# A message-passing kernel: one block per loop body in rounds two and three, its count buffer in seven parts

## The reference

```python
# L0 (round one)
agg = segment_sum(x[src], dst, n);  mean = agg / maximum(deg, 1)[:, None]
h = relu(concatenate([x, mean]) @ W_fc + b_fc) + x @ W_res + b_res
x = layernorm(x + h)
# L1 (rounds two and three), the same conv twice, relu in between
msg = x[src] @ Wm + bm + edge_attr @ We + be
out = segment_sum(msg, dst, n) + x @ Ws + bs
# at the end
x = layernorm(x + out)
```

## Time and profile before

| | |
|---|---|
| timed runs | 4176.44 us median of 3 (4168.92 to 4176.94) |
| profiled execution, first to last instruction | 4128.3 us |
| what lies around it, up to the median of the timed runs | 48.1 us |
| rounds two and three, loops | some 2382 to 3195 us, and 3285 to 4072 us |

### The profile page before, as it was taken

The page is one execution under the profiler, slowest core; times in us unless marked ns, Lnnn a source line. Parts: engine busy times, 40 slices in busy tenths (PEclk is TensorE's granted clock), DMA queues, the critical chain, the costliest instruction groups (busy, mean ns, idle before and its releaser), DMA issues.

```text
span 4128.3 us, 116481 instructions
## 1 busy us (share of the span) xinstructions
PE 3373.4 (82%) x39555; PEld 3061.4 (74%) x39555; DVE 2361.8 (57%) x5334; ACT 1654.2 (40%) x2148; POOL 1962.3 (48%) x2298
## 2 busy tenths in 40 slices
PE   0148899999999995777778888899898789889894
PEld 0137888888888885666667778888888688888884
DVE  7579888898888885777775622222222322222224
ACT  0134577789999995777775400000000300000000
POOL 7722244456666662222221355555554655555552
PEclk9879999999999998999999689999999899999997
DMA  2542355556666664666664389888987798998984
GB/s 94 91 47 104 136 198 209 206 220 248 246 239 241 251 248 157 190 187 187 186 189 126 93 318 334 332 333 328 333 331 280 235 334 326 333 331 326 335 324 148
DMA packets 321181, 967.62 MB, mean 234 GB/s; under 512 B 145354, under 2 KB 238546, under 8 KB 262190
## 3 DMA queue, kind: packets, MB, share of 16 engines
q1 hardware_dynamic: 274338, 893.02, 60.9%
q0 software_dynamic: 46784, 73.84, 6.6%
HBM read 700.07 MB, written 269.81 MB: 235 GB/s over the span
## 4 chain that ended last, share of the span: by engine, by line
PE 64%; DVE 11%; issue 11%; POOL 4%; ACT 4%; DVEq 3%; DMA 2%; ACTq 0%; another core or an unknown queue 0%; POOLq 0%; SPq 0%
PE ps L1060 45%; PE ps L1083 11%; PE ps L1052 4%; DVE union L765 3%; DVE union L878 3%; ACT union L1373 3%; PE ps L1130 2%; DVE abuf L889 2%; POOL abuf L1170 1%; DVEq L439 1%; DVEq L889 1%; PE ps L1020 1%; POOL union L1170 1%; PE ps L974 1%; ACT abuf L1355 1%
## 5 line engine op out<-in xcount | busy, mean ns | idle before, releaser
L1223 POOL DMA_INDIRECT msg<-y_tab,idx x1368 | 1514.4, 1107 | 1373.2 <-ACT idx L1334 859.6
L1060 PE MATMUL ps<-union,abuf 128*128 128x192 bf16 x14896 | 1371.2, 254 | 90.5 <-issue 72.9
L1060 PEld LDWEIGHTS ps<-union,abuf 128*128 128x128 f16 x14896 | 1286.9, 101 | 147.6 <-issue 127.3
L1355 ACT ACTIVATE abuf<-ps 128x784 f16<-128x784 f32 x1216 | 998.6, 824 | 267.5 <-PE ps L1083 237.1
L765 DVE TENSOR_TENSOR union<-lane,union 128x1568 f16<-128x1568 f16 (+3 forms) x1440 | 950.4, 711 | 60.1 <-PE ps L1083 43.9
L1060 PE MATMUL ps<-early,abuf 128*128 128x195 bf16 x7546 | 857.0, 250 | 0.0
L1060 PEld LDWEIGHTS ps<-early,abuf 128*128 128x128 f16 x7546 | 680.0, 100 | 101.3
L1083 PE MATMUL ps<-union 128*128 128x392 f16 (+2 forms) x4288 | 694.1, 290 | 72.5 <-DVE union L765 46.0
L1334 ACT ACTIVATE idx<-src_g 128x6 int32 (+1 forms) x228 | 46.5, 205 | 1566.2 <-PE ps L1052 1035.9
L1130 PE MATMUL ps<-union 128*64 128x128 f32 x7280 | 479.9, 278 | 166.1 <-ACT union L1373 152.0
L1130 PEld LDWEIGHTS ps<-union 128*64 128x64 f32 x7280 | 394.3, 137 | 251.6 <-DVE abuf L889 184.7
(11 more groups left out here) (230 smaller groups left out, 1329.0 us busy)
## 6 DMA issues: line engine op xcount, KB each, us to landing
abuf<-a_dram SPq DMA_DIRECT2D x304, 1568.0 KB
a_dram<-abuf SPq DMA_DIRECT2D x76, 3136.0 KB
union<-in_edge_attr_dram SPq DMA_DIRECT2D x728, 160.0 KB, 2.4
msg<-y_tab,idx POOLq DMA_INDIRECT x1368
y_tab<-union SPq DMA_DIRECT2D x28, 336.0 KB
y_tab<-early SPq DMA_DIRECT2D x7, 682.5 KB
abuf<-x_pad SPq DMA_DIRECT2D x7, 448.0 KB
abuf<-x_pad SPq DMA_DIRECT2D x14, 224.0 KB, 2.8
```

The costliest lines, as they stand in the source:

```text
L1060: last = nc.tensor.matmul(ps[:, bank, 0:3 * width_of[r]], abuf[:, buffer, hi * P:(hi + 1) * P], ycols[r][:, hi, :], start=hi == 0, stop=hi ...
L1223: pool.indirect_dma_start(msg[:, s, 0:3 * width_of[r]], None, y_tab[r], bass.IndirectOffsetOnAxis(ap=idx[:, s:s + 1], axis=0)).then_inc(ga ...
L1355: A.activation(abuf[:, j, :].rearrange("p (h w d) -> p w h d", w=WPB, d=WD) [:, w:w + 2, :, :], ps[:, w % 4:w % 4 + 2, 0:WIN].rearrange("p ...
```

## The change

In rounds two and three a loop body is one block.

- `a_dram` is laid out as 7 parts (`CHUNKS`) of 14 tiles for each block, with rows of 3584 B in place of 12544 B, and round one stores it that way.
- The count buffer is one block, `abuf[:, 0]`, in 7 parts. SyncE loads a part of the next block when TensorE has done with that part of this one. All 7 parts of the first block are loaded in the node phase, whose tiles are moved (`rest` is 64 columns a row wide and no longer 128, `bias_b` goes to the second half of `abuf`).
- The dense sum of a block goes to two PSUM banks: parts 0 to 3 (`FRONT`) to bank 4, parts 4 to 6 to bank 5. VectorE folds and adds each.
- The six gathers are three pieces of two (`PIECE`, `THIRDS`) with one set of six slots of `idx`, `msg` and `hot_g`. Each piece has its own semaphore of arrival and its own PSUM bank (6, 7, 3); TensorE multiplies it after parts 2, 4 and 6. The index copy of a piece waits for the same piece's matmuls of the block before. `hot_g` for the next block is written in one instruction when all three pieces of this block are multiplied.
- GpSimd's wait in the middle of six gathers (`spread`) is gone; it waits once for each piece.

```diff
-        a_dram = [nc.dram_tensor(f"a_dram{j}", [ITERS, 2, P, HALF * P], F16).ap() for j in range(2)]
+        a_dram = nc.dram_tensor("a_dram", [DB, CHUNKS, P, CHUNK * P], F16).ap()
...
+                def d_block(i, mark_next):
+                    before = i * EACH + 1
+                    bs = load_blocks((i + 1) * (GW // 4), GW)
+                    s_add_piece(i, 0, bs, before)
+                    d_add(i, 0, before + PIECE)
+                    s_add_piece(i, 1, bs, before + (PIECE + 1))
+                    if mark_next:
+                        s_mark(i + 1)
+                    d_add(i, 1, before + (2 * PIECE + 1))
+                    s_add_piece(i, 2, bs, before + (2 * PIECE + 2))
...
+                def s_multiply(s, q):
+                    if q == 0:
+                        pe.wait_ge(marked[r], s + 1)
+                    pe.wait_ge(gathered[r][q], s * (16 * PIECE) + 16 * PIECE)
+                    pe.wait_ge(gred[r], s * THIRDS + (q + 1))
+                    for k in in_piece(q):
+                        for c in range(3):
+                            last = nc.tensor.matmul(piece_ps(q, k), hot_g[:, k, :], msg[:, k, c * D:(c + 1) * D],
+                                                    start=c == 0, stop=c == 2)
+                    last.then_inc(gsum[r], 1)
...
-                    for first, end in ((0, GI), (GI, ITERS))[0:1 + (GI < ITERS)]:
-                        with pe.Fori(0, end - first) as i:
-                            for j in range(2):
-                                pe.wait_ge(d_red[j], i + (first + 1 + (r - 1) * ITERS))
-                                for u in range(2):
-                                    pe.wait_ge(a_in[j][u], i * 16 + 16 * (first + 1 + (r - 1) * ITERS))
-                                    dense(j, 4 + j, u * HALF, (u + 1) * HALF).then_inc(a_used[j][u], 1)
-                                if first == 0:
-                                    g_multiply(i, j)
+                    with pe.Fori(0, DB) as i:
+                        for c in range(CHUNKS):
+                            part = int(c >= FRONT)
+                            if c in (0, FRONT):
+                                pe.wait_ge(d_red, i * 2 + (1 + part + (r - 1) * 2 * DB))
+                            pe.wait_ge(a_in[c], i * 16 + 16 * (1 + (r - 1) * DB))
+                            for hi in range(c * CHUNK, (c + 1) * CHUNK):
+                                last = nc.tensor.matmul(ps[:, 4 + part, 0:3 * D], a_buf[:, hi * P:(hi + 1) * P],
+                                                        ycols[r][:, hi, :], start=hi in (0, FRONT * CHUNK),
+                                                        stop=hi in (FRONT * CHUNK - 1, HIS - 1))
+                            last.then_inc(a_used, 1)
+                            if c and c % 2 == 0:
+                                s_multiply(i, c // 2 - 1)
...
+                def s_fetch(s):
+                    for q in range(THIRDS):
+                        pool.wait_ge(staged[r], s * THIRDS + (q + 1))
+                        pool.sem_inc(claimed, 1)
+                        for k in in_piece(q):
+                            pool.indirect_dma_start(msg[:, k, 0:3 * D], None, y_tab[r], bass.IndirectOffsetOnAxis(
+                                ap=idx[:, k:k + 1], axis=0)).then_inc(gathered[r][q], 16)
...
+                def s_stage(s):
+                    for q in range(THIRDS):
+                        act.wait_ge(gsum[r], s * THIRDS + (q + 1))
+                        A.activation(idx[:, q * PIECE:(q + 1) * PIECE], src_g[:, bass.ds(s * G + q * PIECE, PIECE)], ACT.Copy)\
+                            .then_inc(staged[r], 1)
...
+                def a_load(it, c):
+                    sp.wait_ge(a_used, it * CHUNKS + (c + 1 + (r - 1) * CHUNKS * DB))
                     sp.sem_inc(sp_turn, 1)
+                    sp.dma_start(a_buf[:, c * CHUNK * P:(c + 1) * CHUNK * P],
+                                 a_dram[bass.ds(it, 1), c, :, :].rearrange("b p c -> p (b c)"))\
+                      .then_inc(a_in[c], 16)
...
+                    if 0 <= i < CHUNKS:
+                        a_load(0, i)
...
+                with sp.Fori(0, DB - 1) as i:
+                    for c in range(CHUNKS):
+                        a_load(i + 1, c)
```

More of the change, by code:

```diff
@@ L106, in gnn_program @@
     HALF = HIS // 2
+    CHUNKS = 7
+    CHUNK = HIS // CHUNKS
+    FRONT = 4
     G, GW = 6, 8
@@ L466, in _ @@
             dve.sem_inc(e_add, EB)
-            for free in [*d_red, *b_red, *(y for z in gred for y in z), *s_add]:
+            for free in [*b_red, *gred[0], *s_add]:
                 dve.sem_inc(free, 1)
+            dve.sem_inc(d_red, 2)
+            for free in gred[1:]:
+                dve.sem_inc(free, THIRDS)
             dve.wait_ge(s_const, CONSTS)
@@ new lines, in d_add @@
+                def d_add(i, part, before):
+                    upto = (FRONT, CHUNKS)[part]
+                    dve.wait_ge(a_used, i * CHUNKS + (CHUNKS + upto + (r - 1) * CHUNKS * DB))
+                    V.tensor_reduce(part_d[:, part, 0:D], ps[:, 4 + part, 0:3 * D].rearrange("p (c d) -> p d c", c=3),
+                                    AX.X, ALU.add).then_inc(d_red, 1)
+                    dve.wait_ge(d_red, i * 2 + (3 + part + (r - 1) * 2 * DB))
+                    to = feat[:, bass.ds(i + B0, 1), :]
+                    V.tensor_tensor(to, to, part_d[:, part:part + 1, 0:D], ALU.add).then_inc(s_add[r], 1)
+                    dve.wait_ge(s_add[r], before + 1)
```

142 lines of the change are left out of this document (77 added, 65 removed).

## The result

The changed kernel is slower: 4197.72 us median of 6 (4189.64 to 4228.11) against 4168.04 us (4155.92 to 4176.94) on the same chip, a ratio of 1.008 with a 95% interval of 1.0055 to 1.0105. Run again beside the experiments it was 1.014 (1.0106 to 1.0173). The forecast was 4103 us.

The account below looks back on a forecast made before the run. It took TensorE, slowed while the DMA engines are full, to bound the loops' blocks. Blocks at 10.16 us gave -67, edges -6: -73 from 4128.3, span 4055, plus 48 carried over: 4103 us, range 3980 to 4260.

Parts of the forecast that it names:

- What bounds the kernel now: Opening step on the two long loops: 1.80 us of each 10.61 us block lost, TensorE's stream slowing when DMA engines are full.
- wrong in method: Sign of a faulty method: 3584 B packet price off the line, or TensorE's slowing not tied to the DMA engines.
- (a): Count loads, seven of 448 KB for two of 1568 KB: 0.65 us more DMA time a block, 10.16 us in all.
- (b): Finer release of count parts: even requests lift DMA share from 0.90 to 1.0, block 10.16 us, -67 us.
- first rival: DMA share stays at 0.90 in the loops and smaller packets cost: block 11.3 us, +96 us, 4272 us; chance 0.22.
- (c): Gathers in three pieces, one set of buffers: round trip 8.9 us fits in a 10.16 us block, cost nothing.
- second rival: Gathers land in 7.5 us instead of 5.1, TensorE waits; in half the blocks +52, some 4220 us; chance 0.13.
- (d): Second PSUM bank: one more VectorE reduce and add a block, 0.36 + 0.23 us, on an engine 27% busy; cost nothing.
- (e): Edges of the rounds: earlier first gathers and fewer adds at the end, -3 us a round, -6 us together.
- 48 us: Distance of the profiled span below the median of timed runs, added to the forecast span of 4055 us.
- The gaps go: Rival: even requests or a shorter loop body let TensorE run near 9.2 us a block, 3960 us; chance 0.13.
- The clock above 0.94: Sign of being right: TensorE's granted clock in the loops rises above 0.94.

Follow-up runs that it names:

- before_rows1792: The kernel before with each count row of 12544 B cut into seven of 1792 B, same four loads a body; ratio 0.9997.
- before_7parts: The kernel before, two-block buffer and one bank a block kept, with each block's counts in seven loads, waits and releases; ratio 1.0000.
- pieces_only: The kernel before with gathers in three pieces of two and one set of buffers, count buffer and two-block body as before; ratio 1.0040.
- parts_only: The kernel before with the changed kernel's seven-part count loads, release and two banks; gathers and two-block body as before; ratio 1.0049.
- parts_one_bank: parts_only with one PSUM bank a block, by turns, in place of two; ratio to the kernel before 0.9987.
- three_gathers: The kernel before with three gathers a block in place of six, the other three tiles using the first three's rows; ratio 0.9259.
- wide_gathers: The kernel before with one 192-column matmul per gathered tile in place of three of 64, and three more VectorE reductions a block; ratio 0.9971.
- before_cols128: The kernel before with 128 of the 192 columns in each dense matmul of rounds two and three; ratio 0.9928.
- six_in_a_row: The kernel before without GpSimd's wait between a block's third and fourth gather, so six start in one run; ratio 1.0568.

## Why the prediction was wrong

**The bound of a block.** The step that failed is the reading of the short windows in "What bounds the kernel now": "with the DMA engines full for some microseconds, TensorE's stream slows until they have worked off what is queued". The DMA engines were full while TensorE slowed, but GpSimd was starting gathers in the same stretch too. The earlier trace rows have GpSimd at it for 2.3 of the 3.8 us in which TensorE does 20 matmuls, but also for 3.8 of the 6.5 us before, in which TensorE hardly pauses. That these are six starts in one go, and that the slow stretch begins 4.7 us after the first of them (2701.79 to 2706.5), is seen only in GpSimd's timeline. Only kernels that changed one of the two apart from the other could settle it: a share of 0.98 and of 0.60 left the time within 0.7%, half of the starts took 7.4% off. It is what the prediction named as being wrong in method: "if what slows TensorE isn't tied to the DMA engines".

**(a)** came out as forecast: 147 ns a packet forecast, 144 measured; (0.820 + 0.094) x 11.10 = 10.15 us of engine time a block against 10.16. It does not bear on the time.

**(b)** was the term that carried the forecast, -67 us, and it was wrong: nothing was gained where it had a gain. The share stayed at 0.91 and the block went from 10.61 to 11.10 us, +0.49 x 150 = +74 us in these two executions, where the spans differ by 62.9 us (4191.2 - 4128.3) and the medians by 29.7 us. The first rival had "the share stays" and a longer block, but for a reason that has fallen too: its 11.3 us came from the packets, and before_rows1792 has many more of them for nothing. The fixed cost of about 2 us that the prediction takes from the Trainium skill (DMA: Bandwidth & Descriptors, "Anatomy of one DMA") is given there for DMAs that GpSimd starts, while the count loads are SyncE's; seven of them for two cost nothing in before_7parts (1.0000).

**(c)** "Cost nothing" was wrong: TensorE waits 0.4 us a block (27.8 us in 69 blocks), 76 us over both rounds, more than the 50 us that the prediction set as the sign of its second rival. In time it is less, 0.1 us a block by pieces_only. The sum was 8.9 us against a block of 10.16, a cover of 1.2. What it left out is that the index copy starts only when TensorE's signal is through. The third piece shown above is multiplied at 2716.21, and its copy for the next block starts some 3 us later, not 0.4:

```profile
2719.63 0.20 ACT L1414 ACTIVATE idx<-src_g 128x2 int32 x1 [6.17 <-remote]
```

With two blocks to arrive in, the kernel before never waited for it; with one, it uses up the cover of 1.2 us. This is the second rival (0.13) in its effect and not in its reason, which was a later landing; pieces_only puts it at 0.4%, about half of the loss of 0.8%.

**(d)** Whether "nothing" holds is open. The second bank is what distinguishes parts_only (1.0049) from parts_one_bank (0.9987), but those two are from different sets, and that difference is no larger than the one between two measurements of the kernel after. So the half of the loss that is not the gathers' has no shown cause.

**(e)** The start was faster as said (first gathered matmul 10.3 us after the first dense one against 17.1, "within 10 us" forecast). At -6 us in all it is lost in the rest.

**The base.** I carried 48 us around the span. The kernel after has 2.2 us there (4193.4 - 4191.2). The 48 us were the distance of one execution from the median of others; the kernel before has medians from 4118 to 4169 us from set to set. Without the 48 us the forecast would have been 4055 us, so they hid a part of the miss.

**The cases.** "The gaps go" was priced at 9.2 us a block, and three_gathers shows that they can go altogether, 8.67 us; but nothing in this change touched their cause: it starts as many gathers as before, in runs of two of which most join into runs of four. The clock above 0.94, named as a sign of being right, came true in the slower kernel.

A faster kernel came out only in passing: wide_gathers computes the same with 0.3% less, and before_cols128 takes 0.7% off at the price of the third bf16 part. What would pay is fewer starts (the three that three_gathers leaves out are worth 0.64 us a block each on average, some 97 us each over the 152 blocks) or perhaps, as the blocks of 8.81 us with six starts suggest, the same starts with a pause after each three; no run here sets that pause on purpose.

## What to carry to other kernels

When two engines are busy at the same time as a third stalls, a window can't tell which of them does it; halve the work of one and leave the other alone, and look at unnamed "issue" gaps of TensorE beside GpSimd's gather starts as well as beside the DMA share. Count the starts of indirect DMAs as a possible cost to TensorE, look at how long their unbroken runs are, place them in short runs with pauses, and give a fetch that begins on TensorE's signal the lateness of that signal (here 3 us) on top of its own sum. The distance between one profiled execution and a median is no fixed cost to be added.

## What the runs showed of the hardware that was not expected

- While GpSimd starts indirect DMAs, TensorE's signals are late and, after some 4 to 6 us of unbroken starts (at 0.083 us a matmul), its stream stalls: 10.6 us a block with six starts, 8.7 with three, at equal matmuls. In the kernel before runs of three cost 0.2 us each, runs of six 3.3 us each. Rows of 32 B cost as much as rows of 384 B, and three GpSimd subtractions of 128x448 cost nothing.
- It is the report that is late more than the work. In six_in_a_row a signal of the matmul recorded at 2716.72 comes at 2721.80, and that of the matmul recorded at 2723.36, with 48 dense ones of 0.08 us each between them, already at 2723.62, 1.8 us later; 49 matmuls at the recorded pace are 4.0 us.
- The DMA engines can be full (share 0.97 to 1.01, 380 GB/s) for 600 us without costing TensorE anything.
- Seven packets of 1792 B in place of one of 12544 B raise the share from 0.90 to 0.98 and change no time here.
- What stays open: by which resource a gather's start (or its packets) reaches TensorE, how a gather kernel with a pause after each three starts would do, whether the second PSUM bank costs anything, and what the shorter loop body does by itself.
